# A two-layer attention and FFN kernel on one core: weight splitting moved to the FFN stage, large transfers moved behind tile 3's statistics, and k moved ahead of the LayerNorm in tile 2

## What is computed

```
x = x + 0.5 * FFN(layernorm(x))      # two transformer layers: passes 0, L = 0 and 1
x = x + TTT(layernorm(x))            # a recurrent linear attention, not touched here
x = x + 0.5 * FFN(layernorm(x))      # the same two layers again: pass 1, L = 2 and 3
```

```
h = shift_token(x)                   # the upper 128 columns come from the row before
q, k, v = split(h @ wqkv)            # 8 heads of 64
q, k = rotary(l2norm(q) * qs), rotary(l2norm(k) * ks)
x = x + softmax(8 q k^T, window of 128 rows and the 128 before) v @ wo
h = layernorm(shift_token(x)) * ln_g + ln_b
a, g = split(h @ w1 + b1);  x = x + (a * gelu(g)) @ w2 + b2
```

## Time and profile before

| | |
|---|---|
| median of 3 runs | 3043.39 us (3042.09 to 3043.76) |
| the profiled execution | 3048.38 us |
| its span, first to last instruction | 3046.6 us |
| mean granted TensorE clock (1.0 is full speed) | 0.976 |
| PE busy | 2863.3 us (94%) |
| DVE busy | 2256.2 us (74%) |
| ACT busy | 1593.3 us (52%) |
| POOL busy | 1406.0 us (46%) |
| DMA | 76.50 MB, mean 25 GB/s |

### The profile page before, as it was taken

The page is one execution under the profiler, slowest core; times in us unless marked ns, Lnnn a source line. Parts: engine busy times, 40 slices in busy tenths (PEclk is TensorE's granted clock), DMA queues, the critical chain, the costliest instruction groups (busy, mean ns, idle before and its releaser), DMA issues.

```text
span 3046.6 us, 62804 instructions
## 1 busy us (share of the span) xinstructions
PE 2863.3 (94%) x21528; PEld 2428.2 (80%) x21528; DVE 2256.2 (74%) x6572; ACT 1593.3 (52%) x4241; POOL 1406.0 (46%) x1466
## 2 busy tenths in 40 slices
PE   6899999999999999987888899999999999999998
PEld 5788888888888888876666778888888888888887
DVE  7777788877777777746777577777777777777775
ACT  4555555655565556531111155666665555555554
POOL 3444455544444455433322255555555445445443
PEclk8999999999999999998999999999999999999999
DMA  3200000011000000030000000000001100000000
GB/s 105 118 22 29 29 29 22 19 66 53 12 2 2 2 1 2 2 108 24 28 28 28 24 2 2 2 2 2 2 1 50 53 19 16 16 15 15 15 16 22
DMA packets 76858, 76.50 MB, mean 25 GB/s; under 512 B 37648, under 2 KB 63760, under 8 KB 75408
## 3 DMA queue, kind: packets, MB, share of 16 engines
q1 hardware_dynamic: 70784, 71.15, 7.2%
q10 hardware_dynamic: 5776, 1.56, 0.2%
HBM read 48.32 MB, written 23.59 MB: 24 GB/s over the span
## 4 chain that ended last, share of the span: by engine, by line
PE 59%; DVE 17%; issue 13%; ACT 5%; POOL 5%; DMA 0%; DVEq 0%; POOLq 0%; ACTq 0%; SPq 0%
PE bank L865 9%; PE bank L867 9%; PE bank L866 9%; PE bank L1052 8%; PE bank L925 5%; ACT pr L700 4%; PE bank L955 4%; PE bank L941 3%; POOL pr L565 2%; PE bank L901 2%; DVE pr L1268 2%; DVE t L1239 2%; DVE t L1242 2%; DVE h L1327 2%; PE bank L986 2%
## 5 line engine op out<-in xcount | busy, mean ns | idle before, releaser
L565 POOL TENSOR_TENSOR pr<-pr,rden 128x512 f32<-128x512 f32 (+1 forms) x512 | 471.6, 942 | 992.6 <-DVE rden L1277 988.2
L700 ACT ACTIVATE pr<-pr,nb 128x256 f32<-128x256 f32 (+1 forms) x1024 | 478.9, 469 | 274.9 <-DVE nb L1268 272.0
L1052 PE MATMUL bank<-w,uT 128*128 128x256 f32 (+1 forms) x1536 | 434.2, 398 | 0.0
L1268 DVE CUSTOM_DVE_ANT_0 pr<-bank,maskb,r 128x256 f32<-128x256 f32 (+1 forms) x1024 | 401.5, 445 | 28.7 <-PE bank L925 17.6
L865 PE MATMUL bank<-h2T,w 128*128 128x256 f32 x1408 | 410.3, 291 | 4.5 <-DVE uT L1336 1.6
L866 PE MATMUL bank<-h2T,w 128*128 128x256 f32 x1408 | 400.0, 284 | 0.0
L867 PE MATMUL bank<-h2T,w 128*128 128x256 f32 x1408 | 399.7, 284 | 0.0
L1336 DVE SCALAR_TENSOR_TENSOR uT<-bank,b,gg 128x256 f32<-128x256 f32 (+1 forms) x384 | 181.8, 480 | 266.4 <-ACT gg L759 172.6
L865 PE MATMUL bank<-wqkv,hT 128*128 128x512 f32 x768 | 328.4, 428 | 5.3 <-DVE nb L1268 2.8
L866 PE MATMUL bank<-wqkv,hT 128*128 128x512 f32 x768 | 305.1, 397 | 0.0
L867 PE MATMUL bank<-wqkv,hT 128*128 128x512 f32 x768 | 303.6, 395 | 0.0
(11 more groups left out here) (202 smaller groups left out, 6327.3 us busy)
## 6 DMA issues: line engine op xcount, KB each, us to landing
wqkv<-wqkv_split SPq DMA_DIRECT2D x18, 512.0 KB, 6.4
w<-w_split SPq DMA_DIRECT2D x3, 2816.0 KB, 9.8
Y<-in_x SPq DMA_DIRECT2D x8, 512.0 KB, 4.6
uT<-in_x SPq DMA_DIRECT2D x8, 512.0 KB, 4.4
out<-Y SPq DMA_DIRECT2D x8, 512.0 KB, 3.4
h<-out SPq DMA_DIRECT2D x8, 512.0 KB, 4.0
stt<-stt SPq DMA_DIRECT2D x224, 3.0 KB
out<-h SPq DMA_DIRECT2D x7, 512.0 KB, 3.8
```

What stands on the lines that cost most here:

```text
L565: e.tensor_tensor(pr[:, 2 * j:2 * j + 2, 0:wide], pr[:, 2 * j:2 * j + 2, 0:wide], rden[:, 2 * j:2 * j + 2].unsqueeze(2).to_broadcast([P, 2 ...
L700: last = e.activation(pr[:, hd, 0:wide], pr[:, hd, 0:wide], ACT.Exp, bias=nb[:, hd:hd + 1], scale=-1.0, accum_out=den[:, hd:hd + 1])
L1052: mm = e.matmul(bank[bk][:, 0:D], uT[0:rows, t // 2, mt, (t % 2) * P:(t % 2 + 1) * P], w2[0:rows, mt, :], start=(mt == 0), stop=(mt == MT ...
L1268: m = e.tensor_tensor_reduce(pr[:, hd, 0:wide], bank[j][:, g * 256:g * 256 + wide], far, r[:, t, 1, place(hd):place(hd) + 1], FAR, ALU.add ...
```

## The change

1. **Splitting beside the FFN products.** The 14 pieces are now split in sequences (0, 0) to (0, 6), two in each, in the FFN stage: even ones in buffer h, odd ones in t1 (the scratch of A1). The first is loaded behind `move_stats` of tile 2, the second behind tile 3's, once all moves of the sequence have landed, the first piece is loaded and A1 of the next sequence has read t1. ACT makes the high part before its gelu table and behind the first gelu of half 1; DVE does beta and the rest behind the first two `U` of half 1; PE does beta behind the W1 jobs 2 of half 0 and 1 of half 1. DVE's A1 of tile 1 now waits in layer 0 for both stores of the sequence before.
2. **Large transfers** wait for the landing of the moves (`stats_moved`): `load_w2`, `load_rest`. `store_layer0` is spread over b = 1, 2, 3 and comes last in its sequence.
3. **The last sums** (`mix`) of layer 3 move from W2 to behind `U` of the FFN stage's half 1; for b = 7 they stay behind W2, in t1, which is loaded in tile 2 of the last sequence.
4. **Tile 2.** k's part of A1 comes ahead of `LN_moments` on DVE and of `LN` on POOL, and the fourth piece of `LN_apply` behind `O` and `A0`.
5. **Layer 0, first pieces.** `split_lo` of pieces 3 to 6 is spread over tiles 0, 1, 2 of (0, 0); the entry LayerNorm's apply over tiles 1 and 2. w2's first load moves behind tile 2's moves.
6. **Start.** The mask counts as a late constant; half of the rotary scaling goes to POOL in one instruction; ACT loads its table early; PE does 24 transposes of the identity into bank 7 before its first work.

```diff
@@ SP
+            def stats_moved(L, b):
+                e.wait_ge(st_moved[1], at(st_moved[1], 16 * 8 * (8 * L + b + 1)))
...
             def sequence(L, b, last=False):
                 if L == LAYERS - 1 and b:
                     load_out(b - 1)
...
                 move_stats(L, b, 2, st_moved[1])
+                if L == 0 and b == 0:
+                    e.wait_ge(wp_lo, at(wp_lo, len(PIECES)))
+                    e.wait_ge(b1_step, at(b1_step, 2))
+                    e.dma_start(w2[:, :, :], ...).then_inc(w2_loaded, 16)
+                for i in next_pieces(L, b)[0:1]:
+                    if b:
+                        e.wait_ge(nx_stored, at(nx_stored, 16 * i))
+                    load_next(i)
+                if L == LAYERS - 1 and last:
+                    load_out(b)
+                move_stats(L, b, 3, st_moved[1])
                 if L % 2 and b == 0:
+                    stats_moved(L, b)
                     load_w2(L)
-                if L == 0 and b:
-                    store_next(next_at(L, b, 2))
-                move_stats(L, b, 3, st_moved[1])
+                for i in next_pieces(L, b)[1:2]:
+                    stats_moved(L, b)
+                    e.wait_ge(nx_loaded, at(nx_loaded, 16 * i))
+                    e.wait_ge(qrot, at(qrot, idx(L, b + 1, 0) + 1))
+                    load_next(i)
+                for i in next_pieces(L, b):
+                    store_next(i)
+                if L == 0:
+                    store_layer0(b)
@@ POOL, A1(L, b, t, LN_of=None): behind the scaling of k
+                if LN_of:
+                    LN(*LN_of)
@@ POOL, start
+            e.tensor_tensor(rot_other, rot_raw, qks[...].to_broadcast([P, NT, 256]), ALU.mult).then_inc(rot_scaled, 1)
@@ ACT, sequence
-                    if t in (0, 2) and next_at(L, b, t) is not None:
-                        next_hi(next_at(L, b, t))
+                for i in next_pieces(L, b)[0:1]:
+                    next_hi(i)
                 table(ACT.Gelu)
...
                     G(L, b, 1, mt)
+                    if mt == 0:
+                        for i in next_pieces(L, b)[1:2]:
+                            next_hi(i)
@@ PE, next_beta(i, b), for pieces of w1
+                    e.wait_ge(xf_done, at(xf_done, idx(0, b - 1, NT - 1) + 1))
+                    e.wait_ge(b1_step, at(b1_step, 2 + KT * j + k))
+                    e.wait_ge(nx_loaded, at(nx_loaded, 16 * i + 16))
@@ PE, start
+            for _ in range(24):
+                e.transpose(bank[7][:, 0:P], ident[:, :], ident[:, :])
@@ DVE, A1
+                if L == 0 and b and t == 1:
+                    e.wait_ge(nx_stored, at(nx_stored, 16 * 2 * b))
...
                     e.tensor_tensor((kr, qr)[i], t1[:, i, :], t2[:, i, :], ALU.add).then_inc(added, 1)
+                    if LN_of and i == 0:
+                        LN_moments(*LN_of)
@@ DVE, W2 and mix
-                if L == LAYERS - 1:
-                    e.wait_ge(xf_done, at(xf_done, n + 1))
-                    e.wait_ge(xo_loaded, at(xo_loaded, 16 * b + 16))
-                    e.scalar_tensor_tensor(h[:, t, :], xt(Y, b, t), 0.5, h[:, t, :], ALU.mult, ALU.add).then_inc(xo_mixed, 1)
+            def mix(b, t):
+                e.wait_ge(xf_done, at(xf_done, idx(LAYERS - 1, b, t) + 1))
+                e.wait_ge(xo_loaded, at(xo_loaded, 16 * b + 16))
+                x = out_buffer(b)[:, t, :]
+                e.scalar_tensor_tensor(x, xt(Y, b, t), 0.5, x, ALU.mult, ALU.add).then_inc(xo_mixed, 1)
@@ DVE, sequence
-                    if t == 2:
-                        LN_moments(L, b, 0)
                     if ahead:
-                        A1(*ahead)
+                        A1(*ahead, (L, b, 0) if t == 2 else None)
                     if t == 2:
-                        LN_apply(L, b, 0)
+                        LN_apply(L, b, 0, 0, 3)
                     O(L, b, t)
                     if ahead2:
                         A0(*ahead2)
+                    if t == 2:
+                        LN_apply(L, b, 0, 3)
                     if ahead:
                         A2(*ahead)
...
                     if prev:
                         W2(*prev, t)
+                    if L == 0 and b == 0 and t < 3:
+                        split_lo(4 + t)
+                        if t == 1:
+                            beta()
...
                     U(L, b, 1, mt)
+                    for i in next_pieces(L, b)[mt:mt + 1]:
+                        next_beta(i)
+                        next_lo(i)
+                    if L == LAYERS - 1 and b and mt < NT:
+                        mix(b - 1, mt)
```

More of the change, by code:

```diff
@@ L852, in _ @@
             e.wait_ge(s_const, at(s_const, 4))
+            table(ACT.Copy)
             for ps in range(passes):
@@ L1053, in W2 @@
                                   w2[0:rows, mt, :], start=(mt == 0), stop=(mt == MT - 1))
-                if hi == MT and tell:
+                if hi == MT:
                     mm.then_inc(w2_ps, 1)
@@ L1064, in fill @@
                         lo = cuts[k] + (t == 0 and k == 0)
-                        nx = next_at(L, b, t) if k == 3 and t in (0, 2) else None
-                        with_beta = nx is not None and NEXT[nx][0] == "w1"
                         if prev and lo < cuts[k + 1]:
-                            W2(*prev, t, lo, cuts[k + 1], tell=not with_beta)
-                        if with_beta:
-                            next_beta(nx)
+                            W2(*prev, t, lo, cuts[k + 1])
                     S(L, b, t, 0, bool(nxt))
@@ L1101, in sequence @@
                     W1(L, b, 0, mt, bool(nxt))
+                    if mt == 2:
+                        for i in next_pieces(L, b)[0:1]:
+                            next_beta(i, b)
                     if mt == 4:
@@ L1105, in sequence @@
                     W1(L, b, 1, mt, bool(nxt))
+                    if mt == 1:
+                        for i in next_pieces(L, b)[1:2]:
+                            next_beta(i, b)
             def transformer(ps):
@@ L1317, in LN_moments, with LN_apply @@
                 e.tensor_scalar(vare[:, half, 0:w], mv[:, half, 0:w, 1], LN_EPS, None, ALU.add).then_inc(s_pln, 1)
-            def LN_apply(L, b, half):
+            def LN_apply(L, b, half, first=0, end=5):
                 e.wait_ge(mv_done, at(mv_done, 2 * b + (16 * L + half + 1)))
@@ L1322, in LN_apply @@
                 e.wait_ge(h2t_ps, at(h2t_ps, 2 * b + (16 * L + half - 1)))
-                if half == 0:
+                if half == 0 and first == 0:
                     e.tensor_tensor(lead[:, :], mv[:, 0, 0:2, 0], rs[:, 0, 0:2], ALU.mult)
                 for c, t, k in (((4, 1, 1),) if half else ()) + ((0, 2 * half, 0), (1, 2 * half + 1, 0), (2, 2 * half, 1), (3, 2 * half + 1, 1)):
+                    if not first <= c < end:
+                        continue
                     cols = slice(k * DP, (k + 1) * DP)
@@ L1424, in sequence @@
                         R(L, b, t, j)
-                        if L == 0 and t < 2 and b < B - 1:
-                            (entry_stats, entry_apply)[t](b + 1, j)
-                    if L == 0 and b == 0 and t < 2:
-                        for i in ((4,), (5, 6))[t]:
-                            split_lo(i)
-                        if t:
-                            beta()
-                    if t in (1, 3) and next_at(L, b, t) is not None:
-                        next_lo(next_at(L, b, t))
-                    if t == 2:
-                        LN_moments(L, b, 0)
-                    if ahead:
-                        A1(*ahead)
-                    if t == 2:
-                        LN_apply(L, b, 0)
+                        if L == 0 and b < B - 1 and j < 3:
+                            if t == 0:
+                                entry_stats(b + 1, j)
+                            elif t < 3:
+                                entry_apply(b + 1, 2 * t + j - 3)
+                    if L == 0 and b == 0 and t == 0:
+                        split_lo(3)
+                    if ahead:
+                        A1(*ahead, (L, b, 0) if t == 2 else None)
+                    if L == 0 and b < B - 1 and t == 0:
+                        entry_stats(b + 1, 3)
+                    if t == 2:
+                        LN_apply(L, b, 0, 0, 3)
                     O(L, b, t)
@@ L1493, in transformer @@
                     W2(L, B - 1, t, 7 - t)
+                    if L == LAYERS - 1:
+                        mix(B - 1, t)
             def moments(i, src, count):
@@ L1619, in ttt @@
                     normalised(i, tiles(bb, i), tiles(bb, i), 3 * bb + 3 + 2 * more).then_inc(s_ln, 4)
-            def scale_rot(dst, d):
-                for t in range(NT):
-                    out = dst[:, t] if d else dst[:, t, :, :].rearrange("p f d -> p (f d)")
-                    m = e.tensor_tensor(out, rot_raw[:, t, :], qks[:, d * 256:(d + 1) * 256], ALU.mult)
-                m.then_inc(rot_scaled, 1)
             give_credits(e, 2)
```

137 lines of the change are left out of this document (66 added, 71 removed).

## The result

The changed kernel takes 2955.2 us (median of 4 runs, 2953.62 to 2956.40) against 3042.89 for the kernel before on the same chip. The ratio is 0.9711, 95% interval 0.9695 to 0.9728: 87.7 us less. I had forecast 2966.9 us, 76.5 us less, and a range of 2943 to 2994. The two profiled executions stand 92.0 us apart (3048.38 and 2956.40 us), and so do their spans; the terms of the sum are measured against these.

What follows compares the result with a forecast made beforehand. PE, busy 94% of the span, was taken as the bound, so gains came from its lost time. Terms by sequence window, against a clean sequence of 78.54 us afterwards, summed to 76.5 us: 3043.39 to 2966.9 us, range 2943 to 2994.

Steps and rivals of the forecast that it cites:

- start: Kernel start up to the first score: A0 later, A1 at full clock; net 1.0 us less, bounds -3 and +2.
- (0, 0): First sequence of layer 0: two applies instead of four in tile 1, shorter h2 stall; 6.6 us less, bounds 3 to 11.
- (0, 1) to (0, 3): Three sequences of layer 0: from 252.30 us to 3 x 78.94, so 15.5 us less.
- (0, 4) to (0, 6): Three sequences of layer 0: from 251.39 us to 3 x 78.94 plus 5.8 for beta, so 8.8 us less.
- (1, 7): Last sequence of layer 1: a stall of 3 us gone, with tile 2's gain 3.5 us less.
- (2, 0): First sequence of layer 2: 0.5 us less.
- (3, 7): Last sequence of layer 3: 1.1 and 0.5, together 1.6 us less.
- The moves' landing: Statistics' moves in tile 3: with nothing large issued before they land, PE's h2 stall (33.0 us) goes in all 20 places.
- Tile 2: Tile 2 of each sequence: k ready before PE, O for WO next late; 0.5 us less per sequence, bounds 0 and 1.2.
- The beta products: PE's 44 products, in b = 4 to 6 of layer 0 afterwards: 0.13 us each, 5.8 us in all, remaining on PE's path.
- The entry LayerNorm and the second piece: Layer 0: applies in tiles 1 and 2 cost 0.4 us per sequence (bounds 0 and 1.2); piece and store waits cost nothing.
- From the profiled execution to the median: Whole kernel: the same 76.5 us taken from the profiled 3048.38 us (2971.9) and the median 3043.39 us (2966.9).

## Why the prediction was right

Its direction and mechanisms held, and the time lay in the range. By its own terms, forecast and measured gain in the profiled executions:

| term | forecast | measured |
|---|---|---|
| start | 1.0 | 2.2 |
| (0, 0) | 6.6 | 8.4 |
| (0, 1) to (0, 3) | 15.5 | 16.5 |
| (0, 4) to (0, 6) | 8.8 | 12.1 |
| (0, 7), (1, 0) | 12.3 | 12.8 |
| layer 1, b = 1 to 6 | 3.0 | 4.1 |
| (1, 7) | 3.5 | 6.6 |
| TTT part | 0 | 0.2 |
| (2, 0) | 0.5 | 0.9 |
| layer 2, b = 1 to 6 | 3.7 | 5.2 |
| (2, 7), (3, 0) | 7.8 | 8.4 |
| layer 3, b = 1 to 6 | 12.2 | 13.7 |
| (3, 7) | 1.6 | 1.2 |
| the sum | 76.5 | 92.0 |

- **The moves' landing** was right, and it was tested: large transfers close behind cost 0.5 to 2.5 us of stall, and the wait for the landing takes it away at no cost that the windows show. Of the 20 places of PE's wait the one in (2, 0), 1.1 us, stayed beside that in (0, 0); I had taken it as gone. That the clock drops with the longer stalls was right too.
- **(1, 7)** was mis-sized. I counted the stall (3 us) and tile 2, but not the half clock behind them. PE's idle time fell by 3.5 us (8.23 to 4.77), as I had counted, and its busy time by another 3.1, which I had not. The two windows of (1, 7) up to its last FFN product, before and after:

```profile
1270.77:1367.20 96.43, 88.20 (x634) 73.38 (x633) 55.52 (x173) 46.06 (x124) 37.35 (x40) 0.96 0.23 80
```
```profile
1214.76:1304.63 89.87, 85.10 (x634) 70.81 (x633) 54.74 (x173) 46.07 (x124) 36.68 (x40) 1.00 0.24 86
```

  For the other sequences I had taken whole windows, and there, from (0, 1) on and but for beta, the forecast fits within 0.4 us per sequence; here I took a wait, which is just what I had warned of.
- **Tile 2** was mis-sized by my caution: 0.5 us, between bounds of 0 and 1.2, and 0.71 measured. The step was right in its parts: k early, the lead 0.15, O the next bound, a small wait at WO. I placed O's start 0 to 0.6 us earlier; it is 0.7 earlier against its tile. Over 31 sequences this makes 6.5 us of the 15.5 that were missing.
- **The beta products** were mis-sized: I took 0.13 us from start to start and 5.8 us in all; without them 3.5 us are gone, 0.08 each. (The 44 are PE's records; the program has 22 such products, so a product costs 0.16 us.)
- **The entry LayerNorm and the second piece** were charged 0.4 us per sequence; the sequences of layer 0 take 78.6 against 78.3, 0.3. Neither DVE's wait for the stores nor ACT's for the piece appears.
- **(0, 0)** came near, 8.4 against 6.6, but partly by luck. PE's idle time fell by 3.5 us (12.23 to 8.77); the other 5.0 are its busy time at a clock of 0.94 instead of 0.86, and that moves from execution to execution: versions whose (0, 0) differs at most in the order of tile 2 have it at 86.8 to 90.5 us, at clocks of 0.89 to 0.94. Nor did the working give my term: for tile 3 and FFN, 3.8 less 1 less 1 is 1.8, where I wrote 2.6. The scores came late behind the splits about as priced (PE waits 4.5 us there for nb, against 1.4 before). The term of (3, 7) can't be judged at all, since that window moves by 3 us with its clock.
- **The start**: I had the transposes costing as much as they give. They give about 0.6 to 1.2 us. Where the rest of the 2.2 us comes from stays open: no run takes the mask, ACT's table and DVE's half of the scaling apart. I feared that POOL's scaling would block a split; it blocked DVE's own scalings.
- **From the profiled execution to the median** I subtracted the same amount. The kernel before was profiled in an execution 5.5 us above its median, the changed one in one 1.2 above, so 92.0 in the profiles is 87.7 in the medians. Before's runs spread from 3039 to 3048 us over the comparisons, so this part is chance. The 11.2 us between the forecast of 76.5 and the 87.7 in the medians are the 15.5 of the terms less these 4.3.

## What to carry to other kernels

Compare stages of equal work by whole windows first: what the slow ones exceed the clean one by is the gain to be had, with the clock's share in it, which the list of waits leaves out. A small DMA on which a chain hangs should have landed before a large one is issued (tested here with the large one on SP's queue), and work that must be done somewhere belongs into the stage in which its engine has idle time ahead of each instruction. When a wait is removed from a full list, the next one can stand close behind it, here 0.4 us: look for it in the order of that list, and try the pieces one by one.

## What the runs showed that I had not expected

A transfer of 256 KB right behind the small moves costs 0.46 us and one of 768 KB 2.54 us of stall at the same place. A product with one moving column costs PE 0.16 us (two records of 0.08) in a stream of others. 24 transposes at the start raised the clock for the products behind them. A 2-column operation of DVE took 1.00 us beside a scaling of POOL and 0.15 without it, and four scalings of DVE took 3.60 us beside one of POOL and 1.43 alone. POOL was slower beside DVE too: k's scaling took 1.43 us where it started (995.01) inside DVE's sum of two SBUF tiles (994.84, 0.69 long), and 1.04 us where no such sum ran beside it; no run tests this alone.
